# Attention scores in two halves: the products with k's low part on 64 rows, behind the products with k's high part

## The chip, the core and the metric

The kernel runs on one core of a Trainium2 chip. The metric is the device time of one launch in microseconds (us). Three runs of the kernel before gave 1413.69, 1414.14 and 1414.88 us; the median is 1414.14 us.

## The reference

The input x has 8 images of 512 tokens and 1024 features. Each image passes through an attention sublayer and a feed-forward sublayer; both are normalised before and after and added to x. Of the attention this matters:

```
qkv = layernorm(x) @ w_qkv.T + b_qkv          # q, k, v: 512 wide, 8 heads of 64
scores = einsum('bhfc,bhtc->bhft', k, q)      # f: key token, t: query token
scores = where(f <= t, scores, -10000)
attn = softmax(scores, axis=-2)               # over the keys f
vals = einsum('bhft,bhfc->bhtc', attn, v)
out = vals @ w_o.T + b_o
```

The masked entries stay in the softmax with the value -10000, so for every query the keys after it count only through that constant. All values are float32.

## The kernel before

The program is written in two phases, one after the other on each engine. The attention phase handles image by image: seven images in a loop (`body`) and the last one written out (`last_body`). The output phase then does the output projection, the feed-forward product and the norms.

**Precision by splitting.** The tensor engine reads its operands in a rounded form of float32. To keep the precision, a matrix is split into a high part (the rounded value) and a low part (the rest, itself rounded), and a product of two matrices is done as high with high, high with low and low with high. A projection of one pair of heads is 24 such products with 512 moving columns (8 slices of the features by 3).

**Operands of the scores.** A head has 64 channels, and the array has 128 rows, so both parts of q fit beside each other. For the pair of heads p and the head s of the pair (0 or 1), `qst[p % 2][:, s, :]` holds q's high part on the head's own 64 rows (rows 0 to 63 for s = 0, rows 64 to 127 for s = 1) and q's low part on the other 64 rows (`q_hi`, L1104, on ScalarE and `q_lo`, L740, on VectorE). `kst[p % 2][:, s, 0, :]` holds k's high part on both halves of the rows and `kst[p % 2][:, s, 1, :]` k's low part on both: `k_hi` and `k_lo` write the own half, and two DMAs (`dup_k`, L401, queue of SyncE) copy it to the other half.

**The scores of a head (`scores`, L1539).** The 512 queries are four blocks i of 128, and block i needs only the keys of blocks 0 to i: (i + 1) * 128 moving columns. The stationary operand is q's block i with 128 rows (`qst`, loaded by one weight load for each product), the moving one is k. For each i there are two products into the same place of PSUM: part 0 with k's high part on all 128 rows (q high by k high plus q low by k high) and part 1 with k's low part on all 128 rows (q high by k low plus q low by k low). That makes 8 products and 8 weight loads for each of 64 heads (8 images by 8 heads), with 128, 128, 256, 256, 384, 384, 512 and 512 moving columns. The last one raises the semaphore `s_done`.

In PSUM, `ps_s` is three banks of 512 columns. Block 3 fills the first, block 2 takes 384 columns of the second, and blocks 1 (256 columns from 1024) and 0 (128 columns from 1408) share the third (`PS_OFF`, L146). A column beside a block (`FLOOR`) holds the masked constant, for the maximum.

**After the scores.** VectorE waits for `s_done`, writes the mask (`scores_mask`, L780) and takes the negated maxima (L798); ScalarE does the exponentials (`exps`, L1128) and raises `exp_done`; GpSimd normalises (L583); DMAs move the result to a buffer of the rounded type (`move_p`, L412); TensorE transposes it (`transpose_p`, L1390), and after a split into high and low part multiplies it by v (`values`, L1362).

**Order on TensorE.** The order of the instructions is written out by hand. `body` has ten slots for an image. Slot h holds pieces of the projections of this image and the next (L1503, L1497, L1534), the scores of one head, the values of head h - 2 and the transposes of head h - 1. The scores of heads 1, 2, 3, 6 and 7 stand at the end of the slot before theirs (`AHEAD`), those of head 4 behind a projection (`BEHIND`), those of heads 0 and 5 at the start of their slots. The scores wait for `exp_done` of the head before (the same PSUM place), and in an even head also for `q_low` and `k_dup`.

Of the kernel before, what the change touches and what calls it, by code (L numbers as in the profile page):

```python
# [14 lines left out]
P = 128  # L15
# [111 lines left out]
def attention_phase(nc, whole, x, wqkvT, bqk, bv, valsT, wl_late, vals_stored, ps_o, C, W, woT, bo, wagT, BT, gb):  # L127
# [4 lines left out]
    HD = 64  # L132
# [3 lines left out]
    NT = S // P  # L136
# [49 lines left out]
    with ExitStack() as ctx:  # L186
# [18 lines left out]
        kst, qst = [], []  # L205
# [1214 lines left out]
        def tensor(pe):  # L1420
# [118 lines left out]
            def scores(h, b, behind=False):  # L1539

                H, p, s = 8 * b + h, h // 2, h % 2
                if h % 2 == 0:
                    pe.wait_ge(q_low, 4 * b + p + 1)

                    pe.wait_ge(k_dup[p % 2], 32 * (2 * b + p // 2 + 1))
                if h > 0:

                    pe.wait_ge(exp_done, H)
                if behind:

                    pe.wait_ge(x_raw, 8 * b + 5)
                for i in range(NT):
                    for part in range(2):
                        last = pe.matmul(ps_s[:, PS_OFF[i]:PS_OFF[i] + (i + 1) * P],  # L1554
                                         qst[p % 2][:, s, i * P:(i + 1) * P],
                                         kst[p % 2][:, s, part, 0:(i + 1) * P],
                                         start=(part == 0), stop=(part == 1), skip_group_check=True)
                last.then_inc(s_done, 1)

            def tile_product(n, half, ks):  # L1560
# [46 lines left out]
            def body(b):  # L1607
                for h in range(SLOTS):
                    if h < NH and h != BEHIND and h not in AHEAD:
                        scores(h, b)  # L1610
# [6 lines left out]
                    if h == BEHIND:  # L1617
                        scores(h, b, True)
# [21 lines left out]
                    if h + 1 in AHEAD:  # L1640
                        scores(h + 1, b)
# [944 lines left out]
```

## Time and profile before

| What | Value |
|---|---|
| Median of three runs | 1414.14 us |
| Time of the profiled execution | 1414.13 us |
| Its span, from the first instruction to the last | 1412.3 us |
| TensorE matmul (PE) busy | 1396.6 us (99%), 7796 products |
| TensorE weight load (PEld) busy | 1247.1 us (88%), 7796 loads |
| VectorE busy | 1046.3 us (74%) |
| ScalarE busy | 692.8 us (49%) |
| GpSimd busy | 704.1 us (50%) |
| Granted clock of TensorE, mean | 0.999 |

PE rows are products, PEld rows the loads of the stationary operand. A product's row begins when it is issued and ends at a modelled end, so successive rows overlap; the pace of the engine is read from the distance between the starts, not from the durations. The product phase of the attention runs from about 30 to 815 us, the output phase from there to the end.

### The profile page before, as it was taken

What the parts mean: (1) busy time and instruction counts of PE and PEld (TensorE: products, weight loads), DVE (VectorE), ACT (ScalarE), POOL (GpSimd) and SP (SyncE); (2) the same over time, 40 slices, a digit from 0 to 9 for tenths busy, and PEclk for the clock granted to TensorE, in tenths of its full rate; (3) what the DMA queues carried; (4) which work ended last, traced back from release to release, by engine and by line L of the source; (5) the groups of instructions that cost most, each with busy time, mean ns of one, the idle gap of its engine ahead of it and who ended that gap; (6) DMA issues with size and microseconds to landing.
All of it is one profiled execution on the core that took longest, in us unless ns stands there. A gap on an engine that the chain in (4) does not pass through costs nothing.

```text
span 1412.3 us, 25002 instructions
## 1 busy us (share of the span) xinstructions
PE 1396.6 (99%) x7796; PEld 1247.1 (88%) x7796; DVE 1046.3 (74%) x2204; ACT 692.8 (49%) x1498; POOL 704.1 (50%) x1268
## 2 busy tenths in 40 slices
PE   7999999999999999999999999999999999999998
PEld 6888888888888888888888889999999999999997
DVE  7676685776775776766756888898878787878764
ACT  6365465564573664654654764433333333333332
POOL 3364462571562553644624775555555555555542
PEclk9999999999999999999999999999999999999999
DMA  7434334324433343343333643322222222222311
GB/s 253 142 127 120 143 104 154 134 95 138 145 111 123 126 137 138 115 127 138 112 99 94 213 139 116 104 107 98 96 92 101 104 104 91 90 94 96 119 75 60
DMA packets 71797, 168.55 MB, mean 119 GB/s; under 512 B 7760, under 2 KB 31568, under 8 KB 71760
## 3 DMA queue, kind: packets, MB, share of 16 engines
q1 hardware_dynamic: 71760, 168.09, 35.3%
q8 instruction: 19, 0.31, 0.1%
q14 instruction: 18, 0.15, 0.0%
HBM read 62.15 MB, written 25.69 MB: 62 GB/s over the span
## 4 chain that ended last, share of the span: by engine, by line
PE 91%; issue 3%; POOL 2%; DVE 1%; POOLq 1%; ACT 1%; DMA 1%; DVEq 1%; SPq 0%; ACTq 0%
PE ps_f L2471 23%; PE ps_o L1503 21%; PE ps_o L1534 12%; PE ps_s L1554 6%; PE ps_o L2356 6%; PE ps_v L1370 6%; PE ps_t L1408 3%; PE ps_o L1497 3%; PE ps_z L2356 2%; PE ps_f L2417 2%; PE ps_o L1573 2%; PE ps_x L2407 1%; PE ps_v L1378 1%; PE ps_t L1503 1%; PE ps_o L1454 1%
## 5 line engine op out<-in xcount | busy, mean ns | idle before, releaser
L2471 PE MATMUL ps_f<-wagh,x2Th 128*128 128x364 f32 x756 | 250.9, 332 | 0.0
L2471 PE MATMUL ps_f<-wagh,x2Tl 128*128 128x364 f32 x756 | 248.7, 329 | 0.0
L2471 PE MATMUL ps_f<-wagl,x2Th 128*128 128x364 f32 x756 | 248.3, 329 | 0.0
L1503 PE MATMUL ps_o<-xTh,wh 128*128 128x512 f32 x424 | 172.3, 406 | 0.0
L1503 PE MATMUL ps_o<-xTh,wl 128*128 128x512 f32 x424 | 166.5, 393 | 0.0
L1503 PE MATMUL ps_o<-xTl,wh 128*128 128x512 f32 x424 | 165.7, 391 | 0.0
L583 POOL TENSOR_SCALAR pr<-pr,nwm,rden 128x512 f32<-128x512 f32 (+3 forms) x256 | 159.7, 638 | 11.3 <-issue 11.3
L559 POOL TENSOR_TENSOR cw<-wm,cnt 128x4 f32<-128x4 f32 x64 | 12.8, 200 | 300.3 <-ACT pr L1134 300.3
L2471 PEld LDWEIGHTS ps_f<-wagh,x2Th 128*128 128x128 f32 x756 | 142.0, 188 | 2.2 <-issue 0.3
L2471 PEld LDWEIGHTS ps_f<-wagl,x2Th 128*128 128x128 f32 x756 | 142.3, 188 | 1.5
L2471 PEld LDWEIGHTS ps_f<-wagh,x2Tl 128*128 128x128 f32 x756 | 142.3, 188 | 0.0
L736 DVE TENSOR_TENSOR PT<-ps_t,PT 128x512 fp32r<-128x512 f32 (+1 forms) x192 | 110.6, 598 | 35.0 <-ACT PT L1091 31.9
L1134 ACT ACTIVATE pr<-ps_s,nm 128x128 f32<-128x128 f32 (+3 forms) x256 | 130.8, 523 | 0.2
L1091 ACT ACTIVATE PT<-ps_t 128x512 fp32r<-128x512 f32 (+1 forms) x192 | 95.2, 530 | 57.3 <-PE ps_t L1408 51.9
L1901 POOL TENSOR_TENSOR small<-small,eps 128x1 f32<-128x1 f32 x90 | 20.7, 230 | 198.2 <-DVE small L1981 183.6
L798 DVE TENSOR_REDUCE nm<-ps_s 128x1 f32<-128x129 f32 (+3 forms) x256 | 108.0, 484 | 2.2
L1534 PE MATMUL ps_o<-wh_v,xTh 128*128 128x512 f32 x256 | 100.5, 393 | 0.0
L1534 PE MATMUL ps_o<-wh_v,xTl 128*128 128x512 f32 x256 | 99.9, 390 | 0.0
L1503 PEld LDWEIGHTS ps_o<-xTh,wl 128*128 128x128 f32 x424 | 79.6, 188 | 17.9
L1554 PE MATMUL ps_s<-kst,qst 128*128 128x128 f32 (+3 forms) x512 | 94.0, 326 | 0.0
L2227 ACT ACTIVATE f<-f,small 128x512 f32<-128x512 f32 x62 | 47.2, 809 | 95.2 <-POOL small L1905 95.2
L1503 PEld LDWEIGHTS ps_o<-xTl,wh 128*128 128x128 f32 x424 | 79.8, 188 | 14.0
(309 smaller groups left out, 3438.3 us busy)
## 6 DMA issues: line engine op xcount, KB each, us to landing
p_words<-pr SPq DMA_DIRECT2D x56, 448.0 KB, 2.8
kst<-kst SPq DMA_DIRECT2D x64, 256.0 KB, 3.7
x<-in_x SPq DMA_DIRECT2D x31, 512.0 KB, 3.9
x2r<-x2n SPq DMA_DIRECT2D x30, 512.0 KB, 2.9
xs<-in_x SPq DMA_DIRECT2D x24, 512.0 KB, 4.6
out<-x SPq DMA_DIRECT2D x23, 512.0 KB, 2.7
p_words<-pr SPq DMA_DIRECT2D x56, 192.0 KB, 2.3
xs_words<-xs SPq DMA_DIRECT2D x21, 512.0 KB, 3.2
```

Source lines behind the costliest of these rows:

```text
L583: done = pool.tensor_scalar(at, at, nwm[:, q, i:i + 1], rden[:, q, i:i + 1], ALU.add, ALU.mult)
L736: dve.tensor_tensor(LOW_GROUPS[g].rearrange("p (n c) -> p n c", n=n), ps_t[g % 2][:, 0:n * P].rearrange("p (n c) -> p n c", n=n), HIGH_GRO ...
L798: last = dve.tensor_reduce(nm[:, q, i:i + 1], ps_s[:, lo:hi], AX.X, ALU.max, negate=True)
L1091: act.activation(HIGH_GROUPS[g], ps_t[g % 2][:, 0:n * P].rearrange("p (n c) -> p n c", n=n), ACT.Copy)\
L1134: last = act.activation(pr[:, q, S_OFF[i]:S_OFF[i] + n], ps_s[:, PS_OFF[i]:PS_OFF[i] + n], ACT.Exp, bias=nm[:, q, i:i + 1], accum_out=acc[ ...
L1370: pe.matmul(ps_v[:, j * P:], v[:, j, h, :], rows, start=(j == 0 and rows is HIGH_ROWS[0]), stop=False, skip_group_check=True)
L1503: done = pe.matmul(ps[:, :], w[:, k, c:c + P], xT[:, k, :], start=(k == 0 and w is wh and xT is xTh), stop=(k == KD - 1 and w is wl), skip ...
L1534: done = pe.matmul(ps_j[t % 2][:, :], xT[:, k, t * P:(t + 1) * P], w, start=(k == 0 and xT is xTh and w is w_high), stop=(k == KD - 1 and ...
L1554: last = pe.matmul(ps_s[:, PS_OFF[i]:PS_OFF[i] + (i + 1) * P], qst[p % 2][:, s, i * P:(i + 1) * P], kst[p % 2][:, s, part, 0:(i + 1) * P], ...
L2227: return act.activation(out_, in_, ACT.Identity, scale=rstd[r], bias=shift[r])
L2356: last = pe.matmul(bank, a[:, room, k, :], w[part][:, k, :], start=(start and k == 0 and a is rooms_h and part == 0), stop=(stop and k == ...
L2471: last = pe.matmul(ps_f[:, g, 0:GW], a[:, k, :], w[:, k, cols], start=(k == 0 and a is xh and w is wagh), stop=False, skip_group_check=True)
```

## The change

The loops over the block and the part change places: first the four products with k's high part, then the four with k's low part. The products with the high part keep their 128 rows. Those with the low part read only the head's own 64 rows of `qst` and `kst`, the rows on which q's high part stands: rows 0 to 63 for the first head of a pair and 64 to 127 for the second. So the product of q's low part with k's low part is no longer computed. The number of products, weight loads, moving columns and waits stays as it was, and `dup_k` still copies both parts.

The start flag, which makes a bank's earlier content void, is now given for the blocks 0, 2 and 3 of the high part only. Block 1 shares its bank with block 0, whose high product stands ahead of it and whose low product now comes after it.

```diff
-                for i in range(NT):
-                    for part in range(2):
+                own = slice(0, HD) if s == 0 else slice(HD, P)
+                for part, rows in ((0, slice(0, P)), (1, own)):
+                    for i in range(NT):
                         last = pe.matmul(ps_s[:, PS_OFF[i]:PS_OFF[i] + (i + 1) * P],
-                                         qst[p % 2][:, s, i * P:(i + 1) * P],
-                                         kst[p % 2][:, s, part, 0:(i + 1) * P],
-                                         start=(part == 0), stop=(part == 1), skip_group_check=True)
+                                         qst[p % 2][rows, s, i * P:(i + 1) * P],
+                                         kst[p % 2][rows, s, part, 0:(i + 1) * P],
+                                         start=(part == 0 and i != 1), stop=(part == 1), skip_group_check=True)
                 last.then_inc(s_done, 1)
```

## Rows read from the trace of the kernel before

**Rows 1.** The profile's page: span, busy time by engine, granted clock.
```profile
span 1412.3 us, 25002 instructions
PE 1396.6 (99%) x7796; PEld 1247.1 (88%) x7796; DVE 1046.3 (74%) x2204; ACT 692.8 (49%) x1498; POOL 704.1 (50%) x1268
PEclk9999999999999999999999999999999999999999
```

**Rows 2.** The page's chain that ended last, shares by engine.
```profile
PE 91%; issue 3%; POOL 2%; DVE 1%; POOLq 1%; ACT 1%; DMA 1%; DVEq 1%; SPq 0%; ACTq 0%
```

**Rows 3.** Busy time by stretch: window, its length, each engine's busy (count), clock.
```profile
30.00:130.00 100.00, 100.00 (x537) 85.07 (x536) 71.34 (x143) 57.01 (x140) 48.22 (x97) 1.00 0.40 129
130.00:730.00 600.00, 599.97 (x3277) 511.28 (x3276) 417.64 (x834) 339.02 (x841) 290.31 (x593) 1.00 0.39 128
730.00:815.00 85.00, 85.00 (x436) 72.58 (x435) 59.84 (x122) 52.52 (x121) 43.14 (x70) 1.00 0.43 131
```

**Rows 4.** Groups by line and shape: the score products; count, busy us, mean ns.
```profile
L1554 PE MATMUL ps_s<-kst,qst 128*128 128x512 f32 x128 | 40.1, 394 | 0.0
L1554 PE MATMUL ps_s<-kst,qst 128*128 128x384 f32 x128 | 32.8, 338 | 0.0
L1554 PE MATMUL ps_s<-kst,qst 128*128 128x256 f32 x128 | 28.9, 306 | 0.0
L1554 PE MATMUL ps_s<-kst,qst 128*128 128x128 f32 x128 | 23.5, 265 | 0.0
```

**Rows 5.** Timeline of the products about one head: start us, duration us, engine, line.
```profile
205.37 0.39 PE L1497 MATMUL ps_o<-xTl,wh 128*128 128x512 f32 x1
205.60 1.44 PE L1554 MATMUL ps_s<-kst,qst 128*128 128x128 f32 x8
206.88 0.28 PE L1408 MATMUL ps_t<-ident_words,p_words 128*128 128x128 f32 x2
```

**Rows 6.** Timeline of the weight loads of that head, one by one, and the next.
```profile
205.38 0.19 PEld L1554 LDWEIGHTS ps_s<-kst,qst 128*128 128x128 f32 x1
205.60 0.19 PEld L1554 LDWEIGHTS ps_s<-kst,qst 128*128 128x128 f32 x1
205.71 0.19 PEld L1554 LDWEIGHTS ps_s<-kst,qst 128*128 128x128 f32 x1
205.82 0.19 PEld L1554 LDWEIGHTS ps_s<-kst,qst 128*128 128x128 f32 x1
205.94 0.19 PEld L1554 LDWEIGHTS ps_s<-kst,qst 128*128 128x128 f32 x1
206.06 0.19 PEld L1554 LDWEIGHTS ps_s<-kst,qst 128*128 128x128 f32 x1
206.24 0.19 PEld L1554 LDWEIGHTS ps_s<-kst,qst 128*128 128x128 f32 x1
206.41 0.19 PEld L1554 LDWEIGHTS ps_s<-kst,qst 128*128 128x128 f32 x1
206.64 0.14 PEld L1408 LDWEIGHTS ps_t<-ident_words,p_words 128*128 128x128 f32 x1
206.88 0.14 PEld L1408 LDWEIGHTS ps_t<-ident_words,p_words 128*128 128x128 f32 x1
```

**Rows 7.** Timeline where a head's first load does not start with the product ahead.
```profile
185.89 0.39 PE L1503 MATMUL ps_o<-xTh,wl 128*128 128x512 f32 x1
186.27 1.11 PEld L1554 LDWEIGHTS ps_s<-kst,qst 128*128 128x128 f32 x8 [0.41 <-issue]
186.28 1.53 PE L1554 MATMUL ps_s<-kst,qst 128*128 128x128 f32 x8
```

**Rows 8.** The waits of the weight loads: line, what they waited for, us, times, longest.
```profile
PEld ps_s L1554 <- issue: 2.9, 7, 0.4
PEld ps_v L1370 <- issue: 1.4, 7, 0.2
PEld ps_t L1408 <- DVE PT L736: 1.2, 7, 0.2
```

**Rows 9.** The instructions of line 1554: who waited for them (us, times).
```profile
  DVE hold L785: 5.3, 7
```

## The prediction

> **What bounds the kernel now.** I read the page first: matmul is busy 99% of the span, the granted clock is full in every slice [rows 1], and the chain that ended last is 91% TensorE [rows 2]. Since a busy product row can hide an engine that only waits, I then read the busy time by stretch. In the attention phase, where the scores stand, the products cover 100.00 of 100 us, 599.97 of 600 and 85.00 of 85, the weight loads 85% of it, and no other engine is above 72% [rows 3]. The weight loads are where a wait of TensorE would show; on the score line they waited 2.9 us in all, in seven places, one for each turn of the loop, and the next largest waits of this phase are 1.4 and 1.2 us [rows 8]. So TensorE's own pace sets the time of this phase, and what one head's scores gain or lose on TensorE goes into the end nearly one for one, 64 times.
>
> **What a head's scores cost now.** From the start of the first of the eight products (205.60) to the start of what follows (206.88) it is 1.28 us [rows 5]. The distances between the starts of the weight loads show how it is made up: 0.11, 0.11, 0.12, 0.12, 0.18, 0.17, 0.23, 0.24 us [rows 6]. A load starts as the product ahead of it begins (205.38 beside 205.37, 206.88 beside 206.88 [rows 5, 6]) and is hidden under it. The products of 256, 384 and 512 columns so cost 0.12, 0.18 and 0.23 us, in proportion to their columns; the 128-column ones cost 0.11, which is no longer in proportion (a quarter of 0.23 would be 0.06), so there the next load is the limit: a product begins no sooner than 0.11 us after its load started. The mean durations, 0.265 to 0.394 us [rows 4], hold the way through the array and are not the pace.
>
> **The change part by part.**
>
> Columns. The moving columns are the same: 2 x (128 + 256 + 384 + 512) = 2560 for a head. Nothing in the trace makes a product's pace depend on rows, since all 7796 have 128. Term: 0.
>
> Order. In both orders each product is followed by one load, and the cost of each is the larger of its columns and 0.11. Before, the sum is 2 x (0.11 + 0.12 + 0.18 + 0.23) = 1.28 us; in the order 128, 256, 384, 512 twice it is the same 1.28. Both orders end with a 512-column product, so that what follows meets the same neighbour. Block 0 and its twin no longer accumulate into the same place back to back, but at 0.11 us that pair goes at the pace of the load [rows 6], so no stall is there to remove. Term: 0.
>
> Waits and other engines. Waits, the semaphore's place behind the last product, the DMAs of `dup_k`, the mask and the exponentials stay. In one head of eight VectorE waits for the scores, 5.3 us over seven times [rows 9]; it gets later by what the scores get longer and no more, and the next to ask for its result is TensorE, shifted by the same. Term: 0 beyond TensorE's own.
>
> Change of height. This is the new thing. Twice in each head TensorE goes from one height to the other: from a 128-row product of 512 columns (block 3, high) to a 64-row load, and from a 64-row product of 512 columns (block 3, low) to the 128-row load of whatever follows. That is 2 x 64 = 128 changes; the kernel before has none, so the price is bounded from both sides.
> - Lower end, 0: the load starts with the product ahead, as it does between a score product and a transpose of another kind and weight type (206.64, with the last score product [rows 6]).
> - Upper end: the load starts only when the product ahead has left. The trace has one such place for each turn of the loop: the 512-column product of 185.89 is to end at 186.28, and the load of the scores starts at 186.27, with nothing else that it waited for [rows 7]. By the pace of rows 6 the product that this load serves begins 0.11 later, 0.49 us after the one ahead instead of 0.23: 0.26 us lost. 128 x 0.26 = 33.3 us.
> - Between them: the load waits only until the product ahead has taken in its columns (0.23 us for 512), and isn't hidden any more: 0.11 us lost. 128 x 0.11 = 14.1 us.
> - Below nothing: only if a 64-row load were quicker (below).
>
> I take the middle one, 0.11 us: it is what a load costs when it alone loses its cover, it needs no wait for results to leave the array, and it lies between the two rows that the trace has (rows 6 at 0, rows 7 at 0.26), nearer to that of undisturbed loads.
>
> The row says that a load between unlike 128-row instructions goes on under the product ahead. The Trainium skill has a rule on this for changes of height: its page "TensorEngine Tiling (Array Packing)", section Tiling Modes, says "Changing tiling mode (not just tile) drains the TensorE". It gives no time for it. By that rule the term would be one of the two upper values, by the row alone it would be 0. No run here shows a change of height so far, and neither the sum nor its bounds need this sentence.
>
> Sum: in the profiled execution (1414.13 us, span 1412.3, so 1.8 us around it) 14.1 us are added to a phase in which TensorE has no slack: 1428.2 us. The profiled execution stands at the median of the runs shown (1414.14), so no correction is due: 1428 us.
>
> **The rivals.**
>
> A. Changes of height are free, or the 64-row product is run in the full array's arrangement after all, so that there is no change to pay for. For it: of the 7796 loads nearly all start with the product ahead, across kinds and weight types. Against it: none of them changes the rows. Time: 1414.1 us, within 0.1%.
>
> B. Full wait. The load starts when the product ahead has ended by its row, as at 186.27 [rows 7]. For it: that place shows that a wait for an empty array costs just this here. Against it: that place has several semaphore waits ahead of the load, which could be its cause. Time: 1414.1 + 33.3 = 1447.4 us.
>
> C. Exposed loads through the whole low part. If loads into the same 64 rows never go under a product on these rows, the four low products and what follows them pay, five loads for a head: 0.11 behind each of the products of 512 (high), 256, 384 and 512, and behind 128 columns 0.06 + 0.11 instead of 0.11, so 0.06: 4 x 0.11 + 0.06 = 0.50 us, times 64 = 32 us: 1446 us. Against it: 128-row loads go under products on the same rows all through rows 6.
> Beside it, the Trainium skill's page "TensorE: Matmul & The Clock Gate", section Part 3: Packing small matmuls, says that loads overlap running products only where their row groups differ. The trace disagrees for full-height loads (rows 6); for 64-row ones no run here shows it.
>
> D. Faster. A load of 64 rows takes less than one of 128. It decides only where the load is the limit, behind a 128-column product, and there only with a 64-row load next: the low product of block 0 falls from 0.11 to at best its columns, 0.06 us, and only if the load takes less than 0.11. Once for each head: 64 x 0.05 = 3.2 us, and with free changes the time is 1410.9 us. For it: half the rows are half the data. Against it: nothing in the trace; and the changes would have to cost under 0.025 us each, or it is eaten up.
>
> E. Small price. A change costs something, but a fraction of a load, 0.02 to 0.06 us: 3 to 8 us, 1417 to 1422 us. It is the forecast's mechanism in a smaller size.
>
> **How the numbers follow.** Forecast (about 0.11 us for a change, 0.07 to 0.16) 0.32; B and C together 0.20; E 0.14; A 0.28; D 0.06. The predicted time is the forecast's, 1428 us. The range must reach both A and B, which hold much: from 1412 (A, with what runs differ by) to 1449 us (B, with 0.01 us more for a change). Left out are D and prices over 0.27 us, together about 1 in 10. The forecast's own range is 1423 to 1435 us. A difference under 0.2% (2.8 us) can't be told from none. Slower by more than that: forecast, B, C and E but for its lowest end, 0.65; within it: A and that end, 0.29; faster: D, 0.06.
>
> **What would show it.** In the trace of the changed kernel, the distances between load starts in one head give every step. If the forecast is right, the fifth load (the first with 64 rows) starts about 0.23 us after its product ahead began, and so does the first load behind the scores; between them the distances are 0.11, 0.12, 0.18; a head takes about 1.50 us instead of 1.28. In A all loads start with the product ahead and a head takes 1.28. In B it is 1.80, with the two loads at the recorded end of the product ahead. In C every load of the low part is late. D would show a load below 0.19 us and a distance below 0.11. The forecast is wrong altogether if the heads are longer but the time is not (then the phase has slack that rows 3 and 8 don't show), or if the output phase, which the change doesn't touch, moves.

## The result, and the profile after

The changed kernel takes 1438.71 us (median of three runs, 1438.1 to 1439.05) against 1414.14 us before: 24.6 us more. The ratio is 1.0171, with a 95% interval of 1.0154 to 1.0188, so between 21.8 and 26.6 us more. Spread over the 128 changes of height that makes 0.19 us for each (0.17 to 0.21).

The page of the kernel after, its span, busy times and granted clock, answers to [rows 1]:

```profile
span 1436.3 us, 25002 instructions
PE 1420.5 (99%) x7796; PEld 1239.3 (86%) x7796; DVE 1044.7 (73%) x2204; ACT 693.4 (48%) x1498; POOL 704.7 (49%) x1268
PEclk9999999999999999999999999999999999999999
```

The counts are the same, and the clock is full, so nothing is to be laid on it. PE busy grew by 23.9 us with the span (24.0), while PEld busy fell by 7.8. The page alone would say that the products have become slower. Those of 512 and 384 columns haven't, as the groups by line and shape show (count, busy us, mean ns, idle before); they answer to [rows 4]:

```profile
L1555 PE MATMUL ps_s<-kst,qst 128*128 128x512 f32 x64 | 25.4, 397 | 0.0
L1555 PE MATMUL ps_s<-kst,qst 64*128 64x512 f32 x64 | 25.2, 394 | 0.0
L1555 PE MATMUL ps_s<-kst,qst 128*128 128x384 f32 x64 | 21.6, 338 | 0.0
L1555 PE MATMUL ps_s<-kst,qst 64*128 64x384 f32 x64 | 21.4, 335 | 0.0
```

The rows of 256 columns did get longer, from 306 ns [rows 4] to the 334 of the first line below, but they are as long in e1, where no time was lost (the second line), so this comes with the order and costs nothing:

```profile
L1555 PE MATMUL ps_s<-kst,qst 128*128 128x256 f32 x64 | 21.4, 334 | 0.0
L1555 PE MATMUL ps_s<-kst,qst 128*128 128x256 f32 x128 | 42.6, 333 | 0.0
```

The same view for the weight loads of the changed kernel; the number behind the second bar is the time in which the load path stood idle before them:

```profile
L1555 PEld LDWEIGHTS ps_s<-kst,qst 128*128 128x128 f32 x256 | 36.5, 189 | 5.1 <-issue 2.9
L1555 PEld LDWEIGHTS ps_s<-kst,qst 64*128 64x128 f32 x256 | 33.5, 185 | 19.8 <-issue 19.8
```

A 64-row product of 512 columns lasts as long as a 128-row one (394 beside 397 ns), and a 64-row load 185 ns beside 189. What is new is 19.8 us of idle load path before the 64-row loads, 0.31 us in each of 64 heads. The loads that follow the scores have the other half. In the waits of the loads (line, what they waited for, us, times, longest), which answer to [rows 8], they are the lines with 28, 16, 7, 7 and 6 times, 64 in all and 20.0 us:

```profile
PEld ps_s L1555 <- issue: 22.7, 71, 0.5
PEld ps_t L1408 <- issue: 8.7, 28, 0.3
PEld ps_o L1534 <- issue: 5.0, 16, 0.3
PEld ps_o L1503 <- issue: 2.2, 7, 0.3
PEld ps_o L1454 <- issue: 2.2, 7, 0.3
PEld ps_t L1410 <- issue: 1.9, 6, 0.3
```

"Issue" is a wait for nothing that the profile shows: no semaphore holds these loads.

In the head that answers to [rows 5, 6], some loads of the timeline, one by one (start us, duration us, idle before):

```profile
210.00 0.19 PEld L1555 LDWEIGHTS ps_s<-kst,qst 128*128 128x128 f32 x1
210.22 0.19 PEld L1555 LDWEIGHTS ps_s<-kst,qst 128*128 128x128 f32 x1
...
210.45 0.19 PEld L1555 LDWEIGHTS ps_s<-kst,qst 128*128 128x128 f32 x1
210.95 0.18 PEld L1555 LDWEIGHTS ps_s<-kst,qst 64*128 64x128 f32 x1 [0.31 <-issue]
...
211.17 0.19 PEld L1555 LDWEIGHTS ps_s<-kst,qst 64*128 64x128 f32 x1
211.29 0.19 PEld L1555 LDWEIGHTS ps_s<-kst,qst 64*128 64x128 f32 x1
211.78 0.14 PEld L1408 LDWEIGHTS ps_t<-ident_words,p_words 128*128 128x128 f32 x1 [0.31 <-issue]
```

And the two 512-column products that stand ahead of the changes:

```profile
210.62 0.40 PE L1555 MATMUL ps_s<-kst,qst 128*128 128x512 f32 x1
211.46 0.39 PE L1555 MATMUL ps_s<-kst,qst 64*128 64x512 f32 x1
```

The product of 210.62 has taken in its columns at 210.85 (0.23 us, from [rows 6]) and is to end at 211.02. The load behind it starts at 210.95, 0.33 us after the product began: about 0.10 after the last column, and 0.07 before the recorded end. The change back is the same: product at 211.46, load at 211.78, 0.32 us. All heads agree: from the start of the 512-column product to the start of the load behind the change it is 0.316 to 0.325 us on the way to 64 rows and 0.321 to 0.324 us on the way back, for both halves of the rows, against 0.003 us where no height changes. Between the two changes the 64-row loads keep the old pace, 0.12 us from 211.17 to 211.29 behind 256 columns.

All of the difference lies at the scores. From the start of the product ahead of a head's scores to the start of the fifth product behind them, summed over the 64 heads, the traces give 142.0 us before and 166.6 after, 24.6 more.

The phase after the scores did not move: from the last head's scores (809.85 before, 833.43 after) to the end of the span it is 602.5 and 602.9 us, the latter with this head's own two changes in it.

### The profile page after: what moved, and what is told of

Read it like the earlier page. It is cut to its first block, busy times and chain, and to the rows that moved or that the text cites. A ratio compares the mean times of both kernels' runs of the same rounds, so it can differ in the third digit from the quotient of the medians.

```text
span 1436.3 us, 25002 instructions
## 1 busy us (share of the span) xinstructions
PE 1420.5 (99%) x7796; PEld 1239.3 (86%) x7796; DVE 1044.7 (73%) x2204; ACT 693.4 (48%) x1498; POOL 704.7 (49%) x1268
## 4 chain that ended last, share of the span: by engine, by line
PE 91%; issue 3%; POOL 2%; DVE 1%; ACT 1%; POOLq 1%; DVEq 1%; DMA 0%; ACTq 0%
PE ps_f L2472 22%; PE ps_o L1503 21%; PE ps_o L1534 12%; PE ps_s L1555 7%; PE ps_o L2357 6%; PE ps_v L1370 5%; PE ps_t L1408 3%; PE ps_o L1497 3%; PE ps_z L2357 2%; PE ps_f L2418 2%; PE ps_o L1574 1%; PE ps_x L2408 1%; PE ps_v L1378 1%; PE ps_o L1515 1%; PE ps_o L1454 1%
## 5 line engine op out<-in xcount | busy, mean ns | idle before, releaser
L2472 PEld LDWEIGHTS ps_f<-wagh,x2Th 128*128 128x128 f32 x756 | 141.9, 188 | 2.2 <-issue 0.3
L1555 PE MATMUL ps_s<-kst,qst 128*128 128x128 f32 (+7 forms) x512 | 106.9, 338 | 0.1
L1503 PEld LDWEIGHTS ps_o<-xTh,wh 128*128 128x128 f32 x424 | 79.6, 188 | 15.8 <-issue 2.2
```

The source lines that it names most:

```text
L1503: done = pe.matmul(ps[:, :], w[:, k, c:c + P], xT[:, k, :], start=(k == 0 and w is wh and xT is xTh), stop=(k == KD - 1 and w is wl), skip ...
L2472: last = pe.matmul(ps_f[:, g, 0:GW], a[:, k, :], w[:, k, cols], start=(k == 0 and a is xh and w is wagh), stop=False, skip_group_check=True)
```

## The experiments

Each is timed against the kernel before. In the expectations, H is the theory that only the change between 128-row and 64-row instructions costs; its rivals stand with each.

**e1: the order alone.** All eight products on 128 rows, high set first.

```diff
-                own = slice(0, HD) if s == 0 else slice(HD, P)
+                own = slice(0, P)
```

> Only the new order and the new start flags, all eight products of a head on 128 rows. Theory H (each change between 128-row and 64-row instructions costs, nothing else does): no change of height, so 1414 us, and all loads of a head start with the product ahead. Rival O (the order or the accumulation across the two sets of four costs a part): above 1417 us; if it were all of the cost, 1439 us.

Measured: 1412.96 us, ratio 0.9997 (0.9987 to 1.0006). The order and the new start flags cost nothing; rival O is out. From here to the changed kernel only the rows of the low products differ, so the 24.6 us come with them.

**e2: the 64 rows alone.** The order of the kernel before, so that the height changes at each product.

```diff
-                for part, rows in ((0, slice(0, P)), (1, own)):
-                    for i in range(NT):
+                for i in range(NT):
+                    for part, rows in ((0, slice(0, P)), (1, own)):
```

> Only the 64 rows for the products with k's low part; the order is that of the kernel before, high and low in turn for each block, so the height changes 8 times in a head instead of 2. Theory H: by the trace of the changed kernel a load behind a change starts 0.095 us after the product ahead has taken in its columns, and its 0.108 us are no longer hidden, so 0.20 us for a change behind 256, 384 or 512 columns and 0.15 us behind 128 columns (where 0.054 were lost anyway): 6 x 0.20 + 2 x 0.15 = 1.5 us for a head, times 64 = 96 us, 1510 us. Rival R (the cost belongs to the 64-row products themselves, about 0.05 us for each of the eight places, however often the height changes): 1439 us. Rival F (a fixed 0.43 us between a 512-column product and the next, whatever stands ahead): 8 x 0.43 = 3.4 us for a head against 1.28, 1550 us.

Measured: 1510.42 us, ratio 1.0687 (1.067 to 1.0705); 1510 was expected by H, with prices read from the changed kernel's trace, and 1439 and 1550 by its rivals. So the cost goes by the number of changes. That the two numbers agree to 1 us is luck in part: e2's executions had a granted clock of 0.993 to 0.997 against 0.999 before, and by the same sum as above the 64 heads took 92.8 us more, where 96 were expected. The timeline of the loads of one head shows how a change is made up:

```profile
226.77 0.18 PEld L1555 LDWEIGHTS ps_s<-kst,qst 64*128 64x128 f32 x1 [0.18 <-issue]
227.14 0.19 PEld L1555 LDWEIGHTS ps_s<-kst,qst 128*128 128x128 f32 x1 [0.18 <-issue]
227.57 0.18 PEld L1555 LDWEIGHTS ps_s<-kst,qst 64*128 64x128 f32 x1 [0.24 <-issue]
228.00 0.23 PEld L1408 LDWEIGHTS ps_t<-ident_words,p_words 128*128 128x128 f32 x2 [0.24 <-issue]
```

The load of 226.77 is that of block 2's low product, with 384 columns, those of 227.14 and 227.57 are block 3's, high and low, with 512: from 226.77 to 227.14 it is 0.37 us, and from 227.14 to 227.57 and on to 228.00 it is 0.43. Take off the load's 0.11 and the columns at the pace of [rows 6] (0.17 and 0.23), and 0.09 is left both times. Behind 384 and 512 columns alike, a change costs 0.09 us after the columns, plus the load that is hidden no more. It is the same whether the rows go down or up, since 227.57 is a 64-row load and 228.00 a 128-row one.

**e3: a short product ahead of each change.** Blocks 3 to 0 in both sets, so that 128 columns stand ahead of the change.

```diff
-                    for i in range(NT):
+                    for i in reversed(range(NT)):
...
-                                         start=(part == 0 and i != 1), stop=(part == 1), skip_group_check=True)
+                                         start=(part == 0 and i != 0), stop=(part == 1), skip_group_check=True)
```

> As the changed kernel, but the blocks in each set of four run from 3 to 0, so that a 128-column product stands ahead of both changes of height. Theory H with a fixed wait after the columns: 0.15 instead of 0.20 us for a change, 128 x 0.05 = 6.9 us less than the changed kernel, 1432 us. Rival (the wait grows as the product ahead gets shorter, since a fixed time from its start is needed): no gain, 1438 us or more.

Measured: 1429.44 us, ratio 1.011 (1.0093 to 1.0127): 9.3 us below the changed kernel where 6.9 were expected. A part of a change's price is the load's 0.11 us, and behind 128 columns half of that was lost anyway, since such a product doesn't cover a load. The wait is not a fixed time from the product's start, as the product ahead of a change and the load behind it show:

```profile
208.47 0.65 PE L1555 MATMUL ps_s<-kst,qst 128*128 128x128 f32 x2
208.62 0.18 PEld L1555 LDWEIGHTS ps_s<-kst,qst 64*128 64x128 f32 x1
```

It is 0.15 us from the product to the load (0.148 to 0.152 in all heads), and less the 0.06 of its columns the same 0.09 is left. For the 2.4 us too much see e7.

**e4: 96 rows.** In the first head of each pair the low products use rows 0 to 95, in the second all 128.

```diff
-                own = slice(0, HD) if s == 0 else slice(HD, P)
+                own = slice(0, HD + 32) if s == 0 else slice(0, P)
```

> As the changed kernel, but the low products use 96 rows (rows 0 to 95) in the first head of each pair and all 128 in the second; on the 32 additional rows q's low part meets k's low part, as in the kernel before. Theory H in its narrow form (what costs is the arrangement of the array in two halves, and 96 rows still need the whole one): 1414 us. Rival R2 (any change of the number of rows costs): 32 heads x 2 changes x 0.19 us = 12 us, 1426 us.

Measured: 1413.72 us, ratio 0.9998 (0.9988 to 1.0007). The loads by shape:

```profile
L1555 PEld LDWEIGHTS ps_s<-kst,qst 128*128 128x128 f32 x384 | 55.4, 189 | 6.8 <-issue 3.1
L1555 PEld LDWEIGHTS ps_s<-kst,qst 96*128 96x128 f32 x128 | 19.5, 190 | 1.4
```

128 loads with 96 rows stand between 128-row ones, with 1.4 us idle in all. So another number of rows doesn't cost by itself; R2 is out. What costs is going from the whole array to a half and back. Other counts than 128, 96 and 64 were not run, so where between 96 and 64 the price sets in is open.

**e5 and e6: the other half.** The low products of blocks 2 and 3 read the other 64 rows. The first diff is e5's, the second e6's.

```diff
+                own, other = (slice(0, HD), slice(HD, P)) if s == 0 else (slice(HD, P), slice(0, HD))
...
                     for i in range(NT):
+                        rows = other if part == 1 and i > 1 else rows
```

```diff
+                for part, order in ((0, (0, 1, 2, 3)), (1, (0, 2, 1, 3))):
+                    for i in order:
+                        rows = slice(0, P) if part == 0 else (own if i < 2 else other)
```

The other half of `qst` holds q's low part. So in blocks 2 and 3 both leave out q's high part with k's low part: they answer what the time does, and are no replacement for the changed kernel.

> As the changed kernel, but the low products of blocks 2 and 3 read the other 64 rows of the same tiles, so that k's low part meets q's low part there instead of q's high part: this part of the scores is another one. One more change in a head, from one half of the rows to the other, with the height still 64. Theory H (only the change between the whole array and halves costs): nothing is added, 1439 us, and at best the 256-column product of block 1 runs beside block 2's, 0.12 us for a head, 1431 us. Rival (each change of the rows in use waits for the array): 64 x 0.20 = 13 us more, 1452 us.

> As e5, but the low products run in the order of blocks 0, 2, 1, 3, so that the two halves of the rows take turns: blocks 0 and 1 on the head's own rows, 2 and 3 on the others (k's low part by q's low part there). Three changes of half in a head. Theory H: no cost, 1439 us; if the halves work side by side, the 384 columns of blocks 0 and 1 vanish under the 896 of blocks 2 and 3: 0.18 us for a head, 11 us, 1427 us. Rival (each change of rows waits): 3 x 64 x 0.19 = 36 us more, 1475 us.

Measured: 1423.78 us (ratio 1.0067, 1.0052 to 1.0082) and 1423.76 us (1.0064, 1.0049 to 1.0079). Changes from one half to the other add no wait; the rival (1452 and 1475) is out. Moreover the halves work at the same time: e5 is 15 us below the changed kernel, beyond H's best (1431). The loads of e5 about one low set:

```profile
206.58 0.64 PEld L1556 LDWEIGHTS ps_s<-kst,qst 128*128 128x128 f32 x4
207.53 0.30 PEld L1556 LDWEIGHTS ps_s<-kst,qst 64*128 64x128 f32 x4 [0.31 <-issue]
208.14 0.22 PEld L1408 LDWEIGHTS ps_t<-ident_words,p_words 128*128 128x128 f32 x2 [0.31 <-DVE PT L736]
```

The four 64-row loads take 0.30 us together, and from the first of them to the load behind the set it is 0.61 us, against 0.83 in the changed kernel (210.95 to 211.78); 64 x 0.22 = 14 us. Both 0.31 us waits are still there. The next fence says why e5 and e6 are equal, though their programs are not. It has e5's product rows at four moments of the same set; a row begins with the first product still running then, and names that one's shape:

```profile
207.53 0.49 PE L1556 MATMUL ps_s<-kst,qst 64*128 64x128 f32 x3
207.54 0.67 PE L1556 MATMUL ps_s<-kst,qst 64*128 64x384 f32 x3
207.69 0.52 PE L1556 MATMUL ps_s<-kst,qst 64*128 64x256 f32 x2
207.82 0.39 PE L1556 MATMUL ps_s<-kst,qst 64*128 64x512 f32 x1
```

In the program block 1 (256 columns) stands ahead of block 2 (384). On the chip block 2 began first, at 207.54, beside block 0 on the other half; block 1, on block 0's half, began at 207.69, 0.16 us after block 0, which is the 0.11 of block 0's load and the 0.06 of its columns. The starts have this order, block 0, 2, 1, 3, in all 64 heads of e5 as in those of e6.

**e7: e3's order with 128 rows**, as its control; to e3's diff comes e1's line. The same line was changed in three more places, where `k_lo`, `q_hi` and `k_hi` write `kst` and `qst`:

```diff
-                    own = slice(0, HD) if s == 0 else slice(HD, P)
+                    own = slice(0, P)
```

There VectorE and ScalarE now write 128 rows at a time instead of the head's 64; `q_lo` and `dup_k` then put the other half right. So e7 is not as pure a control as its expectation says. These instructions last about as long as before (mean 747, 685 and 688 ns beside 750, 683 and 679), but no run separates what they do to the time.

> Control for e3: its order (blocks 3 to 0 in each set of four), but all eight products on 128 rows. Theory H: this order is free in itself, 1414 us, and all of e3's gain over the changed kernel (9.3 us, where 6.9 were expected) comes from the changes of height. Rival: the order itself gives 2 us or more, 1412 us or less, which would be the missing 2.4 us and a version faster than both.

Measured: 1412.33 us, ratio 0.9987 (0.9978 to 0.9996): some 2 us (0.6 to 3.1) faster than before. It is the fastest of all, and the only version clear of no change on the fast side. e3 against e7 is 17.1 us for 128 changes, 0.13 us each. Summed over the heads as above, the traces give 158.8 us in e3 and 141.0 in e7. So at the scores e3 wins 7.8 us over the changed kernel and e7 0.9 over e1 (141.9), and without these 0.9 e3's gain is the 6.9 that were expected. What is left, 1.5 us of e3's 9.3 and about 1 of e7's 2, lies outside the scores and is no more than executions of one kernel differ by (1412.7 to 1415.2 us for the kernel before). The waits of e7's loads:

```profile
PEld ps_s L1555 <- issue: 2.3, 7, 0.4
PEld ps_t L1431 <- POOL xs L552: 1.0, 1, 1.0
PEld ps_o L1515 <- DVE wl L1036: 0.7, 2, 0.5
PEld ps_o L2357 <- DVE y L2103: 0.7, 1, 0.7
```

Of the three waits of [rows 8], the first is 0.6 us smaller and the other two, 1.4 and 1.2 us, are not on its list. The first accounts for most of the 0.9 us at the scores. The other two don't explain the rest: the list of e3 has neither, and a wait of the load path costs nothing while a product covers it. Whether there is a rest to explain is open.

## Why the prediction was right in kind and short in size

**What bounds the kernel: right.** The phase had no slack. The load path stood 0.31 us before 128 loads, and the time took all of what that costs: the 24.6 us are those by which the 64 heads got longer.

**Columns and order: right.** e1 shows 0 for the order.

**Waits and other engines: right.** VectorE waits for the scores 6.9 us in seven heads instead of 5.3 [rows 9], which costs nothing by itself.

**Change of height: the mechanism was right, the size short.** The term was 128 x 0.11 = 14.1 us; it measured 24.6, or 0.19 for a change. That is above the forecast's own 0.07 to 0.16 us, and 1438.71 us is above its own range of 1423 to 1435. The time lies in the wide range only because that was drawn to reach B, and prices between 0.16 us and B's 0.26 had no chance of their own. The forecast had the load start once the product ahead has taken in its columns. It starts 0.09 to 0.10 us after that, so the term should have been 128 x (0.11 + 0.09) = 25.6 us; 35 changes back (the 28 and 7 loads of L1408 and L1454 above) lead into transposes, whose loads need only 0.08 us (two of 0.14 in 0.22 us, the row of 208.14 under e5), which takes off 35 x 0.03 and brings it to about 24.6. (The 6 loads of L1410 belong to transposes too, but start 0.11 us apart.) The step that failed is the choice "nearer to that of undisturbed loads", which took 0.11 out of 0 to 0.26. The wait needed "for results to leave the array", which the forecast did without, may exist in part: the load starts 0.09 us behind the columns, and a product's row outlasts them by 0.16 (its end is modelled). What the load waits for in these 0.09 us, no run shows. The truth lay between the middle and the upper bound. Had the prediction taken the middle of the two upper values, 0.185 for a change, it would have said 1437.8 us.

The Trainium skill's rule ("TensorEngine Tiling (Array Packing)", Tiling Modes), that a change of the tiling mode and not just of the tile drains TensorE, fits what the runs show: the whole array to a half and back has the wait (e2), another number of rows has not (e4), and another half has not (e5, e6). The runs put the number to it, 0.09 us and the load.

**Rivals.** A (free) is out by the result. B (1447) took the place at 186.27 [rows 7] for its measure; a change costs three quarters of it, and the place itself is another matter, since in the changed kernel it is still there, without a change of height, and the change that follows in the same head has its own wait behind it:

```profile
190.07 0.52 PEld L1555 LDWEIGHTS ps_s<-kst,qst 128*128 128x128 f32 x4 [0.45 <-issue]
190.91 0.18 PEld L1555 LDWEIGHTS ps_s<-kst,qst 64*128 64x128 f32 x1 [0.32 <-issue]
```

C (exposed loads through the low part) is out: 64-row loads between the changes go under products on the same rows, as at 211.17 and 211.29, so the rule of the Trainium skill's page "TensorE: Matmul & The Clock Gate" (Part 3: Packing small matmuls) that was weighed with C doesn't hold here either. D (a quicker load) is out: 185 beside 189 ns, and no smaller distance. E (0.02 to 0.06 us) was too small. By the signs named ahead, a head should have gone from 1.28 to about 1.50 us; it is 1.56 from the first product to what follows (210.22 to 211.78), and 0.08 more of it comes after, with the first load behind the scores that is no longer hidden.

## What to carry to other kernels

Going between instructions that need the whole array and ones that fit into half of it costs TensorE a wait (here 0.09 us behind the last column) and the cover of the next load (0.11 us), so group such products, count the changes rather than the products, and put a short product ahead of each change. Half the rows made neither a product nor a load cheaper here; what they won, they won when the other half worked at the same time: low products on both halves at once gave back 15 of the 24.6 us and still lost. Where loads are never idle, a trace tells such a stall by idle time of the load path put down to nothing, not by the products' rows.

## What the runs showed of the hardware that was not expected

- The price of a change does not come with any other number of rows: 96 rows beside 128 cost 0 (e4), 64 beside 128 cost 0.19 us.
- Products on different halves of the rows run at the same time, begun within 0.01 us of each other (207.53 and 207.54), and a product whose half is free begins ahead of an earlier one in the program whose half is busy (384 columns at 207.54, 256 columns at 207.69). Here the last product of the set, which raises the semaphore, also has the most columns; whether such a semaphore is enough where an earlier product is longer, no run shows.
- The place where the scores of head 4 wait 0.4 us for nothing that the profile shows stayed in every version; its cause is open.
